# Attention tile in pairs of score banks, and x1 normalised by ScalarE in two operations instead of by VectorE in one

## The reference

```python
def _L0_attn_ref(x, Wqkv, bqkv, Wo, bo):
    qkv = jnp.einsum('bsc,cf->bsf', x, Wqkv) + bqkv
    ...
    attn = jax.nn.softmax(jnp.einsum('bqd,bkd->bqk', q, k) * scale, axis=-1)
    out = jnp.einsum('bqk,bkd->bqd', attn, v)
    return jnp.einsum('bqd,dc->bqc', out, Wo) + bo
...
x = x + _layernorm(_L0_attn_ref(_layernorm(x), ...))
x = x + _layernorm(_L0_ffn_ref(_layernorm(x), ...))
```

## Time and profile before

| | |
|---|---|
| median of three executions | 1657.61 us |
| the profiled execution | 1659.3 us |
| its span | 1657.5 us |
| granted PE clock in the attention stage | 1.00 |
| PE busy, whole span | 1634.2 us (99%) |
| DVE busy | 1125.3 us (68%) |
| ACT busy | 620.7 us (37%) |
| POOL busy | 480.4 us (29%) |
| start of scores of tile 9, of tile 10 | 283.11, 299.04 us |

### The profile page before, as it was taken

One profiled execution on the slowest core, in us unless ns is written; L12 is line 12 of the kernel. 1 busy time (PEld: TensorE's weight loads), 2 busy tenths in 40 slices (PEclk: granted clock), 3 DMA queues, 4 the chain that ended last, 5 costly groups with the idle time before them and its releaser, 6 DMA issues.

```text
span 1657.5 us, 20772 instructions
## 1 busy us (share of the span) xinstructions
PE 1634.2 (99%) x7528; PEld 1357.2 (82%) x7528; DVE 1125.3 (68%) x1641; ACT 620.7 (37%) x1117; POOL 480.4 (29%) x409
## 2 busy tenths in 40 slices
PE   7999999999999999999999999999999999999998
PEld 6888888888788888888888888888888888888886
DVE  7865788987766566565557867855555555654676
ACT  3222443345433322333246544322322333244561
POOL 3330554554354544454201102412211111200003
PEclk9999999999999999999999999999999999999999
DMA  7541557659565455655489765744444554487772
GB/s 295 203 178 61 207 179 228 221 185 285 191 210 158 160 175 190 191 174 165 159 261 319 240 202 189 260 142 140 139 148 142 166 158 145 140 289 247 225 261 102
DMA packets 185061, 320.29 MB, mean 193 GB/s; under 512 B 32384, under 2 KB 59136, under 8 KB 183680
## 3 DMA queue, kind: packets, MB, share of 16 engines
q1 hardware_dynamic: 184960, 318.97, 58.7%
HBM read 215.35 MB, written 103.56 MB: 192 GB/s over the span
## 4 chain that ended last, share of the span: by engine, by line
PE 90%; DVE 4%; DMA 2%; SPq 1%; issue 1%; ACT 1%; POOL 0%; DVEq 0%; ACTq 0%; POOLq 0%
PE ps L349 27%; PE ps L351 27%; PE ps L350 27%; PE ps L2012 3%; PE ps L1908 2%; PE ps L2013 1%; PE ps L1957 1%; DMA w_raw<-hsp_dram 1%; PE ps L1958 1%; DVE y_all L1828 1%; DVE norm_x_stats L1340 0%; SPq L568 0%; SPq L584 0%; DMA xc_raw<-xq_dram 0%; DMA x_tile<-x 0%
## 5 line engine op out<-in xcount | busy, mean ns | idle before, releaser
L1359 DVE TENSOR_TENSOR slots<-w_raw,slots 128x512 fp32r<-128x512 f32 x500 | 407.2, 834 | 267.2 <-ACT slots L1170 267.0
L1170 ACT CAST slots<-w_raw 128x512 fp32r<-128x512 f32 x504 | 302.1, 620 | 472.1 <-PE ps L351 446.9
L349 PE MATMUL ps<-xc,slots 128*128 128x512 f32 x1208 | 470.2, 389 | 4.0 <-issue 4.0
L351 PE MATMUL ps<-xc,slots 128*128 128x512 f32 x1208 | 470.0, 389 | 0.0
L350 PE MATMUL ps<-xc,slots 128*128 128x512 f32 x1208 | 469.9, 389 | 0.0
L349 PEld LDWEIGHTS ps<-xc,slots 128*128 128x128 f32 x1208 | 226.7, 188 | 51.7 <-issue 4.8
L351 PEld LDWEIGHTS ps<-xc,slots 128*128 128x128 f32 x1208 | 226.7, 188 | 47.3
L350 PEld LDWEIGHTS ps<-xc,slots 128*128 128x128 f32 x1208 | 226.7, 188 | 46.9
L349 PE MATMUL ps<-slots 128*128 128x512 f32 x560 | 218.0, 389 | 0.1
L350 PE MATMUL ps<-slots 128*128 128x512 f32 x560 | 217.9, 389 | 0.0
L351 PE MATMUL ps<-slots 128*128 128x512 f32 x560 | 217.8, 389 | 0.0
(11 more groups left out here) (194 smaller groups left out, 2362.5 us busy)
## 6 DMA issues: line engine op xcount, KB each, us to landing
w_raw<-hsp_dram SPq DMA_DIRECT2D x154, 256.0 KB, 4.0
hsp_dram<-hs SPq DMA_DIRECT2D x20, 1792.0 KB, 8.3
w_raw<-wffn SPq DMA_DIRECT2D x134, 256.0 KB, 3.7
w_raw<-wffn SPq DMA_DIRECT2D x58, 512.0 KB, 6.1
w_raw<-wdt_dram SPq DMA_DIRECT2D x88, 256.0 KB, 3.9
wgt_dram<-tt SPq DMA_DIRECT2D x21, 1024.0 KB, 8.3
w_raw<-wgt_dram SPq DMA_DIRECT2D x84, 256.0 KB, 2.7
xc_raw<-xq_dram SPq DMA_DIRECT2D x36, 256.0 KB, 5.1
```

Of the source, the lines that this page charges most:

```text
L349: pe.matmul(dst, stat(HIGH), mov(HIGH), start=first, stop=False, skip_group_check=reread)
L351: return pe.matmul(dst, stat(LOW), mov(HIGH), start=False, stop=last, skip_group_check=reread)
L1170: act.copy(operand(n, HIGH), source(n)).then_inc(w_high, 1)
L1359: return dve.tensor_tensor(dst, src, high.bitcast(F32), ALU.subtract)
```

## The change

On PE, the scores of banks 0 and 1 are made together, then the output of t-2 and both groups of probabilities are transposed, then the same for banks 2 and 3. On DVE the two maxima of a pair come first, then the copies of both groups. The normalising of x1 goes to ACT as two operations, after the exponentials: the mean is subtracted, then the result is scaled. DVE in its place negates the mean, one value per row. And `x1_blocks` moves, on DVE, from ahead of the first half of the output projection to between `o_out` and `a_norm`.

```diff
+            def x1_normed(u):
+                act.wait_ge(x1_mean_negated, u + 1)
+                if u > 0:
+                    act.wait_ge(cols_ready, u)
+                act.activation(x1n[:, 0, :], x1_of(u), ACT.Identity, bias=neg_mean[:, 0:1]).then_inc(x1_centred, 1)
+                act.wait_ge(x1_centred, u + 1)
+                act.wait_ge(norm_l.rstd_done, u + 1)
+                act.activation(x1n[:, 0, :], x1n[:, 0, :], ACT.Copy, scale=norm_l.rstd[:, 0:1]).then_inc(x1n_done, 1)
...
                 exponentials(t)
+                if 3 <= t < TILES - 1:
+                    x1_normed(t - 3)
...
                     if u > 0:
-                        dve.wait_ge(cols_ready, u)
-                    dve.wait_ge(norm_l.rstd_done, u + 1)
-                    dve.tensor_scalar(x1n[:, 0, :], x1_of(u), norm_l.moments[:, 0, 0:1], norm_l.rstd[:, 0:1],
-                                      ALU.subtract, ALU.mult).then_inc(x1n_done, 1)
+                        dve.wait_ge(x1_centred, u)
+                    dve.wait_ge(norm_l.moments_done, u + 1)
+                    dve.tensor_scalar(neg_mean[:, 0:1], norm_l.moments[:, 0, 0:1], -1.0, None,
+                                      ALU.mult).then_inc(x1_mean_negated, 1)
...
                 invert_sum(t - 1)
-                if t >= 2:
-                    ot_split(t - 2)
-                for g in range(4):
-                    maximum(t, g)
-                    pt_split(t - 1, g, 4 + g % 2)
-                    if 3 <= t < last:
-                        x1_norm(t, g)
+                for pair in ((0, 1), (2, 3)):
+                    for g in pair:
+                        maximum(t, g)
+                    if t >= 2 and pair[0] == 0:
+                        ot_split(t - 2)
+                    for g in pair:
+                        pt_split(t - 1, g, 4 + g % 2)
+                        if 3 <= t < last:
+                            x1_norm(t, g)
...
-                    if 3 <= t < last:
-                        x1_blocks(t - 3)
                     a_out(t - 2, 0)
...
                 o_out(t - 1)
+                if 3 <= t < last:
+                    x1_blocks(t - 3)
                 if 2 <= t < last:
                     a_norm(t - 2)
...
-                for g in range(4):
-
-                    pe.wait_ge(exp_done, t * 4 + (g - 3))
-                    scores(t, g)
-                    if older and g == 0:
-
+                for pair in ((0, 1), (2, 3)):
+                    for g in pair:
+                        pe.wait_ge(exp_done, t * 4 + (g - 3))
+                        scores(t, g)
+                    if older and pair[0] == 0:
                         transpose_output(t - 2)
-                    if g > 1:
-                        pe.wait_ge(pt_low, t * 4 + (g - 5))
-                    elif not older:
-                        pe.wait_ge(v_summed, TILES - TPB + 1 + g)
-                    transpose_probs(g, 4 + g % 2)
+                    for g in pair:
+                        if g > 1:
+                            pe.wait_ge(pt_low, t * 4 + (g - 5))
+                        elif not older:
+                            pe.wait_ge(v_summed, TILES - TPB + 1 + g)
+                        transpose_probs(g, 4 + g % 2)
```

More of the change, by code:

```diff
@@ L316, in transformer_block @@
     x1_stored, x1n_done = sem("x1_stored"), sem("x1n_done")
+    x1_mean_negated, x1_centred = sem("x1_mean_negated"), sem("x1_centred")
     cols_ready = sem("cols_ready")
```

## The result

The changed kernel took 1685.06 us in the median of four executions (1684.61 to 1687.37), against 1658.18 us for the kernel before (1657.02 to 1658.79) on the same chip: a ratio of 1.0162, with a 95% interval of 1.0148 to 1.0176. It is 26.9 us slower. The forecast was 1686.0. The profiled execution of the changed kernel took 1687.37 us, the longest of its four, and has a span of 1685.5, 28.0 above that of before.

A forecast was written before the change was run, and what follows sets the result against it. PE was taken to set the time. DVE's chain 14.9, POOL 7.6 and SP's queue 5.9 sum to 28.4 us, turning the median of 1657.6 into 1686.0; forecast case within 1679 to 1693, overall range 1671 to 1696.

The forecast's parts named there:

- Bound and place: In tiles 2 to 14 PE sets the time; the output projection's first half waits for DVE's third copy of probabilities.
- Grouping on PE, 0: On PE, a group of transposes has no fixed cost, so two groups instead of four save 0.
- The 3.0 us for exposed loads of weights: On PE, each return from a short transpose would expose one load of weights: 3.0 us of gain, an estimate.
- DVE's chain, 14.9: From o_sum to the third copy, tiles 4 to 14: output projection waits 1.35 us each, 14.9 us.
- ACT: On ACT, two operations of 1.05 us each, 2.10 together, fit its idle time; x1n done about T+14.5, o_half not late.
- POOL, 7.6: POOL's deviation behind x1n delays a_norm in tiles 4 to 7, 10 and 11, late weight loads in tile 8: 7.6 us.
- SP at tile 14, 5.9: In tile 14, stores waiting for the moved block transpose hold back the feed-forward input loads: 5.9 us.
- one rival: Only the PE wait counts; loads after the last store catch up in a less full queue: 1672.5 us, chance 0.20.
- The rival "worse": PE's waits around tile 8 or at 438.88 make the granted clock fall, say 12 us: about 1698 us, chance 0.16.

The follow-up runs named there:

- the last experiment: Kernel before with the pairing of banks on PE and DVE alone, plus the statistics of x1 behind the third copy of probabilities: 1659.57 us, ratio 1.0005.
- early blocks in tiles 6 and 14: Changed kernel with the block transpose ahead of the second half of the output projection in tiles 6 and 14 alone: 1680.38 us, ratio 1.0127.
- pairs alone: Kernel before with only the pairing of banks on PE and DVE; x1 stays with DVE, block transpose unmoved: 1660.53 us, ratio 1.0022.
- pairs, statistics behind: Kernel before with the pairing of banks on PE and DVE, and the statistics of x1 behind the third copy of probabilities: 1659.57 us, ratio 1.0005.
- blocks only: Kernel before with x1_blocks moved behind o_out and nothing else: 1673.28 us, ratio 1.0108.
- statistics behind: Changed kernel with the statistics of x1 taken behind the third copy of probabilities instead of ahead of it: 1675.00 us, ratio 1.0114.
- POOL early: Changed kernel with POOL's sums of weights begun when DVE has negated the mean, not waiting for x1n: 1682.60 us, ratio 1.0145.

## Why the prediction was right

**Bound and place.** PE sets the time, and the third copy in front of the output projection is where it waits: shown by the waits (eleven of them), and by the kernel in which 1.19 us less on DVE's chain make tiles 1.19 shorter.

**Grouping on PE, 0.** Right within 1.1 us. Taken as in the prediction, with the matmul behind them and less one step of 0.235, ten transposes take 300.33 - 299.01 - 0.235 = 1.085 us, 0.109 each, as forecast with no fixed cost. The 3.0 us for exposed loads of weights did not come; a load of 128 columns shows as 0.19 us in the rows of these traces and not as 0.107. The 15.85 to 15.91 of the last experiment leave 0.02 to 0.08 a tile, at most 1.1 us over 14 tiles, of which its total keeps nothing.

**DVE's chain, 14.9.** Forecast P0 at T+10.29 and 1.35 a tile; measured T+10.15 and 1.31, so 11 x 1.31 = 14.4. The start was 0.14 early and the slow first step gave 0.10 back, which the rows of before couldn't show, since no projection of theirs came right behind a copy.

**ACT.** x1n was done at 310.76, T+14.54 (14.5 forecast). Two operations took 2.35 and not 2.10; ACT had the room.

**POOL, 7.6.** Measured over 17.24: tiles 4 to 7 (18.11, 17.93, 17.84, 17.93) 2.9 for 2.1, tile 10 0.4 for 0.4, tile 11 1.65 for 1.6, tile 8 3.7 for 3.5; together 8.6. The chain in tile 8 was as foretold: POOL starts its sums at T8+0.42 (forecast T8+0.3), behind a wait of 6.58 for the loads of weights, and a_norm is at T8+6.6, in the timeline of DVE:

```profile
281.93 0.81 DVE L1366 TENSOR_SCALAR x_odd<-x_odd,norm_a_moments,norm_a_rstd 128x1024 f32<-128x1024 f32 x1 [3.44 <-POOL norm_a_rstd L844]
```

and what it does to PE, in PE's timeline:

```profile
285.18 1.04 PE L1922 MATMUL ps<-ident,probs 128*128 128x128 f32 x6 [3.13 <-DVE probs_t L1371]
```

Only the shape differs: PE waits in two pieces, 3.13 here and 1.3 at the projection.

**SP at tile 14, 5.9.** The first half of the step was right, its end only in part. SP's queue in the changed kernel:

```profile
404.92 7.07 SPq L569 DMA_DIRECT2D xq_dram<-x_cols  x8
...
430.77 12.66 SPq L585 DMA_DIRECT2D xc_raw<-xs_dram  x12
...
447.42 4.74 SPq L585 DMA_DIRECT2D xc_raw<-xs_dram  x4
```

and in the timeline of ACT the cast through which the chain of work runs:

```profile
430.95 1.99 ACT L1202 CAST xc<-xc_raw 128x1024 fp32r<-128x1024 f32 x2 [4.24 <-DMA xc_raw<-xq_dram]
432.85 0.46 ACT L1146 ACTIVATE o_half<-ps,inv_sum 128x256 f32<-128x256 f32 x1
```

The queue of SP in the kernel before:

```profile
402.58 12.65 SPq L584 DMA_DIRECT2D xc_raw<-xs_dram  x12
...
418.18 8.17 SPq L584 DMA_DIRECT2D xc_raw<-xs_dram  x4
```

and a load in its chain of work:

```profile
395.72 6.05 DMA xc_raw<-xq_dram
```

Against T15, which came 22.98 later, the load from xq_dram on that chain landed 6.2 late (430.95 against 395.72 + 6.05 = 401.77) and the next twelve were issued 5.2 late. But the last four took 4.74 us to issue in place of 8.17, and the product that stands behind these loads began at 469.01 instead of 442.46: 3.6 late. So this term measured 3.6, not 5.9; the transfers caught up by 2.3, of which one rival had made the whole. The kernel with the early blocks in tiles 6 and 14, which gives back 3.6 behind T15, says the same. Another 1.5 us came later, in waits near 930 and 1083 us that differ from run to run; no term of the prediction had them. The split between the two is less sure than their sum: with the pairs alone and with pairs, statistics behind, where the stores are not moved, this product begins 61.35 and 62.18 us behind T15 (63.75 before, 67.32 changed), while the whole stretch differs by 0.6 at most.

**Sum.** 14.4 + 8.6 - 0.1 (small differences in tiles 1 to 3) + 5.1 = 28.0, the difference of the spans; forecast 28.4. Each term is there, but that the sum fits to 0.4 is luck: the terms were 0.5 too much, 1.0 too little and 2.3 too much, and 1.5 was in none of them.

**The clock.** In the changed kernel it did fall, and it didn't count. A stretch of it (columns as in the earlier trace rows):

```profile
436.00:443.00 7.00, 7.00 (x23) 5.56 (x22) 7.00 (x8) 5.17 (x9) 2.57 (x2) 0.66 1.20 296
```

and the timeline of PE at its start:

```profile
435.56 0.69 PE L1922 MATMUL ps<-ident,o_sum 128*128 128x128 f32 x2 [4.30 <-DVE o_sum L1551]
...
436.48 0.63 PE L351 MATMUL ps<-xc,slots 128*128 128x512 f32 x1
436.90 0.63 PE L352 MATMUL ps<-xc,slots 128*128 128x512 f32 x1
```

ACT takes o_half behind the late casts, so the transposes of the output wait 4.30 us, and the matmuls behind step by 0.43 instead of 0.23 (1.2 for 2.4 GHz) until 440.7. Eleven of them cost some 2.2 us. But the product of 469.01 has to wait for its loads afterwards anyway, and waits 0.66 in place of 3.58. DVE's timeline shows where the way from the last loads goes on:

```profile
459.59 2.36 DVE L1371 TENSOR_TENSOR xc<-xc_raw,xc 128x1024 fp32r<-128x1024 f32 x2 [0.77 <-ACT xc L1202]
```

ACT's cast ahead of it had waited 0.41 for the DMA (1.21 before). From 459.59 on DVE works without a gap of more than 0.05 to 468.92, 0.1 ahead of the product (433.09 to 442.36 before), so PE's slow matmuls are on this way with 0.15 us at most, for which DVE waited at 446.70, ahead of the issue of the last four loads.

The rival "worse" had the mechanism right. In the changed kernel its cost is hidden; in tile 8 with the blocks only and with the statistics behind it is on the path, with 1.5 and 1.6 us, and with POOL early in part. That is far below the 12 us at which the prediction put it: the clock was back after 3 to 7 us each time. What the prediction held against it, that 3.58 us of idle time had left the clock at 1.00, was true of that place (the stretch in the earlier trace rows ends with the wait, but 442 to 448 us show 1.00 too) and no guide to others: 3.50 us brought it down elsewhere.

## What to carry to other kernels

Where one engine is always busy, look at its waits on a shared buffer and add up, row by row, everything that the engine which frees it must do since the last time it was synchronised; that sum came within 0.15 us here. An operation that is moved must be asked two things: who is queued behind it in the new place, and when its input is ready there. The parts of a change aren't additive (55.7 us alone, 26.9 together), so what each wait costs is found by removing it from the whole, and the removals are then to be tried together, as they were here. And a wait on something that doesn't move with the tiles, as the loads behind the stores, grows when the tiles ahead of it get shorter.

## What the runs showed that was not expected

- A matmul whose bank is freed just late starts with a step of 0.33 us in place of 0.23 and costs its block 0.1 us, while the profile shows no wait (1.49 against 1.39 for six).
- PE idle for 3.58 us left the granted clock at 1.00 in the kernel before, and so did 3.13 in tile 8 of the changed one. At half, 1.2 GHz, it was after 4.30 us in the changed kernel, after 4.96 and 3.92 with the blocks only, after 3.94 and 3.80 with the statistics behind, and after 3.50 and 4.09 with POOL early. So near 3.5 us these runs show both outcomes, 3.50 with a fall and 3.58 without. The Trainium skill ("TensorE: Matmul & The Clock Gate", why this matters for your kernels) warns of idle gaps between bursts; the traces agree for seven of these nine gaps.
- The low part of the queries took DVE 1.53 us in tile 9 of the kernel before, beside a POOL instruction on its own operands, and 0.41 in the changed one, where POOL was idle then. DVE's timeline of before:

```profile
295.89 1.53 DVE L1359 TENSOR_TENSOR q_tile<-q_t,q_tile 128x256 fp32r<-128x256 f32 x1
```

POOL's:

```profile
295.85 1.29 POOL L906 TENSOR_TENSOR tt<-w_raw,tt 128x512 f32<-128x512 f32 x1
```

and DVE's of the changed kernel:

```profile
308.77 0.41 DVE L1371 TENSOR_TENSOR q_tile<-q_t,q_tile 128x256 fp32r<-128x256 f32 x1
```

The Trainium skill ("SBUF — State Buffer", section "SBUF: two separate sides") says that a VectorE operation with two SBUF inputs and a GpSimd one that reads SBUF hold a shared pair of ports in turn. The rows agree: the slow one ends 0.28 us behind POOL's, which started 0.04 ahead of it.
